# Two more layer normalisations by VectorE's batch statistics, in a fused macaron block (feed-forward, Mamba, feed-forward)

## The reference, cut to what matters

```python
x = x + 0.5 * ffn(layernorm(x))     # first feed-forward
x = x + mamba(layernorm(x))         # state-space layer
x = x + 0.5 * ffn(layernorm(x))     # second feed-forward, the same weights

def layernorm(x, eps=1e-5):
    return (x - mean(x)) / sqrt(var(x) + eps)
def ffn(x):    # 8 experts, all of them on every row
    cw = softmax(x @ w_router) * softmax(x @ w_gating / 0.1);  cw = cw / (sum(cw) + 1e-9)
    return sum_e cw[e] * ((silu(x @ w_gate[e]) * (x @ w_up[e])) @ w_down[e])   # 128 -> 512 -> 128
def mamba(x):  # 128 -> 256 inner channels, 16 states per channel
    xs, z = split(x @ W_in);  xc = silu(causal_conv4(xs) + conv_b)
    dt, B, C = projections of xc;  dt = softplus(...)
    h[t] = exp(dt[t] * A) * h[t-1] + dt[t] * xc[t] * B[t];  y[t] = h[t] . C[t]
    return ((y + xc * D) * silu(z)) @ W_out
```

## Time and profile before

| | |
|---|---|
| time, median of 3 runs | 1272.25 us (1271.98 to 1272.68) |
| span of the profiled execution | 1272.6 us |
| TensorE (PE) busy | 1253.2 us, 98% |
| VectorE (DVE) busy | 1114.1 us, 88% |
| ScalarE (ACT) busy | 926.6 us, 73% |
| GpSimd (POOL) busy | 394.3 us, 31% |

### The profile page before, as it was taken

The page is one execution under the profiler, slowest core; times in us unless marked ns, Lnnn a source line. Parts: engine busy times, 40 slices in busy tenths (PEclk is TensorE's granted clock), DMA queues, the critical chain, the costliest instruction groups (busy, mean ns, idle before and its releaser), DMA issues.

```text
span 1272.6 us, 21027 instructions
## 1 busy us (share of the span) xinstructions
PE 1253.2 (98%) x7584; PEld 1096.0 (86%) x7584; DVE 1114.1 (88%) x1481; ACT 926.6 (73%) x1778; POOL 394.3 (31%) x459
## 2 busy tenths in 40 slices
PE   7999999999999999999999999999999999999998
PEld 5888888888888888888888888888888888888887
DVE  4544899989999999999999999999999989999433
ACT  5645978978886978877968788798867968654421
POOL 0101333334342423343333433333334333332110
PEclk9999999999999999999999999999999999999999
DMA  8211677777788868787987878887978887895111
GB/s 244 52 26 30 146 155 154 147 154 158 152 180 164 170 132 183 159 165 161 180 177 150 166 164 176 158 168 148 186 157 167 163 165 142 163 183 107 35 33 33
DMA packets 109303, 182.96 MB, mean 144 GB/s; under 512 B 11024, under 2 KB 23824, under 8 KB 109200
## 3 DMA queue, kind: packets, MB, share of 16 engines
q0 software_dynamic: 56336, 102.79, 45.9%
q1 hardware_dynamic: 52864, 78.85, 24.7%
HBM read 76.22 MB, written 2.62 MB: 62 GB/s over the span
## 4 chain that ended last, share of the span: by engine, by line
PE 73%; DVE 8%; DMA 8%; issue 5%; ACT 3%; POOL 2%; SPq 0%; DVEq 0%; POOLq 0%; ACTq 0%
PE PS L700 27%; PE PS L643 14%; PE PS L646 14%; PE PS L644 14%; DMA Y<-HS 5%; DVE HB L825 2%; DVE HS L923 2%; DMA XS<-DX 2%; DVE HS L931 1%; PE PS L730 1%; PE PS L715 1%; DVE HS L912 1%; PE PS L658 1%; POOL Y L1137 1%; DVE YE L818 1%
## 5 line engine op out<-in xcount | busy, mean ns | idle before, releaser
L700 PEld LDWEIGHTS PS<-WD,HB 128*128 128x128 f32 x4096 | 536.6, 191 | 44.0 <-issue 1.5
L700 PE MATMUL PS<-WD,HB 128*128 128x128 f32 x4096 | 540.1, 275 | 0.0
L1016 ACT ACTIVATE HB<-PS 128x512 f32<-128x512 f32 x512 | 294.3, 596 | 272.9 <-PE PS L646 270.8
L825 DVE TENSOR_TENSOR HB<-PS,HB 128x512 f32<-128x512 f32 x512 | 348.7, 682 | 119.2 <-PE PS L646 110.9
L1137 POOL DMA_DIRECT2D Y<-HS x252 | 221.1, 972 | 383.7 <-DVE HS L931 262.7
L1120 POOL DMA_DIRECT2D XT<-YE x126 | 117.9, 936 | 433.2 <-DVE YE L818 407.4
L643 PE MATMUL PS<-XH,WG 128*128 128x512 f32 x512 | 244.5, 478 | 3.3 <-ACT XH L996 2.3
L643 PE MATMUL PS<-XH,WU 128*128 128x512 f32 x512 | 204.9, 400 | 0.0
L646 PE MATMUL PS<-XH,WG 128*128 128x512 f32 x512 | 203.2, 397 | 0.6 <-DVE XH L883 0.6
L646 PE MATMUL PS<-XH,WU 128*128 128x512 f32 x512 | 202.1, 395 | 0.0
L644 PE MATMUL PS<-XH,WG 128*128 128x512 f32 x512 | 201.0, 393 | 0.0
(11 more groups left out here) (109 smaller groups left out, 1080.9 us busy)
## 6 DMA issues: line engine op xcount, KB each, us to landing
BCB<-BCD SPq DMA_DIRECT2D x128, 512.0 KB, 5.3
Y<-HS POOLq DMA_DIRECT2D x252, 256.0 KB, 6.4
XT<-YE POOLq DMA_DIRECT2D x126, 256.0 KB, 4.4
XS<-DX POOLq DMA_DIRECT2D x7, 512.0 KB, 9.2
XT<-in_L_attn_x_dram SPq DMA_DIRECT2D x8, 256.0 KB, 6.5
WD<-in_L_ffn_w_down_dram SPq DMA_DIRECT2D x8, 256.0 KB, 4.8
out_dram<-XT SPq DMA_DIRECT2D x8, 256.0 KB, 5.6
HS<-in_L_ffn_w_gate_dram SPq DMA_DIRECT2D x6, 256.0 KB, 4.0
```

Of the source, the lines that this page charges most:

```text
L700: z = pe.matmul(expert(g)[:, j, :], HB[:, i % NH, j * P:(j + 1) * P], WD[:, e, c, :], start=c == 0 and j == 0, stop=c == FC - 1 and j == S ...
L825: v.tensor_tensor(H, up(i), H, ALU.mult).then_inc(S["v_h"], 1)
L1016: a.activation(HB[:, i % NH, :], gate(i), ACT.Silu).then_inc(S["a_sil"], 1)
```

## The change

`QUICK` names three normalisations: x of tile 0 (which had this form already), x1 of tile 0 (ahead of the first Mamba stage) and x2 of tile 7 (ahead of the last position). These take the form by VectorE's statistics, renamed `ln_quick` and `ln_quick_x`; the other 21 keep ScalarE's form. The quick form does not wait for `calm()` (a ScalarE clock at most 0.9 ahead of TensorE's) before it is planned. The waits are written for a quick normalisation that is not the first: VectorE waits for `a_xn` of the one before, and both writers of XN wait for what last held XN.

```diff
+QUICK = [("x", 0), ("x1", 0), ("x2", NT - 1)]
...
         yield from rows_of_x()
-        yield from calm()
-        if q == 0:
-            at = step("ln_first", b, what, after=4.0, v=1.5, p=1.2)
-            yield "first"
-            at = step("ln_first_x", b, after=at, v=.7, a=.9)
+        if what in QUICK:
+            f = QUICK.index(what)
+            at = step("ln_quick", q, f, b, what, after=clock["pe"] if q else 4.0, v=1.5, p=1.2)
+            yield True if q else "first"
+            if q:
+                yield from until_v(at - .4)
+            at = step("ln_quick_x", q, f, b, xn["by"], after=at, v=.7, a=.9)
         else:
-            at = step("ln_sum", q, b, xn["by"], what, after=clock["pe"], a=1.6)
+            f = None
+            k = q - len([w for w in QUICK if w in normed])
+            yield from calm()
+            at = step("ln_sum", k, b, xn["by"], what, after=clock["pe"], a=1.6)
             yield True
             yield from calm()
-            at = step("ln_square", q, b, after=at, a=1.6, p=2.0)
+            at = step("ln_square", q, k, b, after=at, a=1.6, p=2.0)
             yield from until(at + .3)
-            at = step("ln_x", q, b, after=at, a=1.5)
+            at = step("ln_x", k, b, after=at, a=1.5)
+        normed.add(what)
         ln["lock"] = False
...
-                        if q == 0 and j == 2:
-                            wt.wait_ge(S["v_xn"], 1)
+                        if f is not None and j == 2:
+                            wt.wait_ge(S["v_xn"], f + 1)
...
-                if k == "ln_first":
-                    _, b, what = s
+                if k == "ln_quick":
+                    _, q, f, b, what = s
                     wait_x(wt, what)
+                    wt.wait_ge(S["a_xn"], q)
                     for j in range(SUB):
                         z = v.bn_stats(stats[:, j, :], XT[:, b, j, :])
...
-                elif k == "ln_first_x":
-                    b = s[1]
-                    wt.wait_ge(S["v_nm"], 1)
+                elif k == "ln_quick_x":
+                    _, q, f, b, at = s
+                    wt.wait_ge(S["v_nm"], f + 1)
+                    wait_count(wt, at)
                     for j in range(2):
                         z = a.activation(XN[:, j, :], XT[:, b, j, :], ACT.Identity, bias=nm[:, j:j + 1], scale=rs[:, j:j + 1])
```

More of the change, by code:

```diff
@@ L90, in timetable @@
     prepared = set()
-    norms = [0]
+    norms, normed = [0], set()
     def rows_of_x():
@@ L120, in norm @@
         bk = yield from take()
-        at = step("ln_t", q, bk, pe=.6)
+        at = step("ln_t", q, f, bk, pe=.6)
         xn.update(by=("m_tr", q + 1), lock=False)
@@ L650, in _ @@
                 if k == "ln_t":
-                    _, q, (b, at) = s
+                    _, q, f, (b, at) = s
                     wait_count(wt, at)
@@ L761, in _ @@
                     v.tensor_scalar(ve[:, :], mv[:, :, 1], EPS_LN, None, ALU.add).then_inc(S["v_ve"], 1)
-                elif k == "ln_first_x":
-                    b = s[1]
-                    wt.wait_ge(S["p_rs"], 1)
+                elif k == "ln_quick_x":
+                    _, q, f, b, at = s
+                    wt.wait_ge(S["p_rs"], q + 1)
                     v.scalar_tensor_tensor(out=nm[:, :], in0=mv[:, :, 0], scalar=-1.0, in1=rs[:, :], op0=ALU.mult,
                                            op1=ALU.mult).then_inc(S["v_nm"], 1)
-                    wt.wait_ge(S["v_nm"], 1)
+                    wt.wait_ge(S["v_nm"], f + 1)
+                    wait_count(wt, at)
                     for j in range(2, SUB):
@@ L969, in _ @@
                 elif k == "ln_sum":
-                    _, q, b, at, what = s
+                    _, k, b, at, what = s
                     wait_x(wt, what)
@@ L976, in _ @@
                 elif k == "ln_square":
-                    _, q, b = s
-                    wt.wait_ge(S["a_sum"], q)
+                    _, q, k, b = s
+                    wt.wait_ge(S["a_sum"], k + 1)
                     a.activation(mean[:, :], sums[:, :], ACT.Copy, scale=-1.0 / P).then_inc(S["a_mean"], 1)
-                    wt.wait_ge(S["a_mean"], q)
+                    wt.wait_ge(S["a_mean"], k + 1)
                     for j in range(SUB):
@@ L984, in _ @@
                 elif k == "ln_x":
-                    _, q, b = s
-                    wt.wait_ge(S["p_nm"], q)
+                    _, k, b = s
+                    wt.wait_ge(S["p_nm"], k + 1)
                     for j in range(SUB):
@@ L1097, in _ @@
                 k = s[0]
-                if k == "ln_first":
-                    wt.wait_ge(S["v_ve"], 1)
+                if k == "ln_quick":
+                    f = s[2]
+                    wt.wait_ge(S["v_ve"], f + 1)
                     wt.wait_ge(S["init"], 3)
@@ L1102, in _ @@
                 elif k == "ln_square":
-                    _, q, b = s
-                    wt.wait_ge(S["a_sq"], q)
+                    _, q, k, b = s
+                    wt.wait_ge(S["a_sq"], k + 1)
                     wt.wait_ge(S["init"], 3)
                     gp.tensor_scalar(ve[:, :], squares[:, :], 1.0 / P, EPS_LN, ALU.mult, ALU.add).then_inc(S["p_ve"], 1)
-                    wt.wait_ge(S["p_ve"], q)
+                    wt.wait_ge(S["p_ve"], k + 1)
                     gp.tensor_tensor(rs[:, :], ve[:, :], mhalf[:, :], ALU.pow).then_inc(S["p_rs"], 1)
```

## The result

The changed kernel takes 1276.89 us (median of 5 runs, 1275.72 to 1277.55) against 1272.25 us for the kernel before (5 runs, 1271.13 to 1274.63): ratio 1.0037, 95% interval [1.0024, 1.0049]. That is 4.6 us slower, where 3.9 us faster was forecast, and outside the range. The span of its profiled execution is 1275.6 us against 1272.6. Wherever both are on record, the time of an execution is 1.5 to 2.0 us longer than its span (1277.16 for the span of 1275.6). So the profiled execution of the kernel before took about 1274.2 us, an estimate from its span: it is one of its longer ones, some 2 us above the median and not 0.35. Between the two profiles there are 3.0 us to explain, not 4.6.

A forecast was written before the change was run, and what follows sets the result against it. TensorE was taken as bound, with the last position's normalisation bounding a few microseconds; removing the last boundary's 3.86 us, plus 0 for x1 of tile 0 and 0 for VectorE's queue, gave 1272.25 - 3.86 = 1268.4 us, range 1265.4 to 1273.0.

The forecast's parts named there:

- the 3.86 us of the last boundary: Between positions 14 and 15: waits for XN (0.97) and XH (0.69) plus about 2.2 us of half clock, all expected to go.
- the 5.46 us of the prediction's own sum: TensorE's time without waits between the two gate products around the last boundary, summed from starts; it needed 9.32 us.
- The 2.2 us for the clock: Rest of the last boundary's cost, laid to TensorE at 1.2 GHz against 2.4 after the two pauses.
- The quick form's length and the transposes' place: x2 of tile 7: quick form takes 4.2 us, and its transposes move about one slot ahead, before the last down product.
- The cost of nothing in VectorE's queue: Some 1.3 us of statistics ahead of one product in each changed place, costed at nothing; without cover at most 1.3 each.
- The normalisation of x1 of tile 0: Ahead of the first Mamba stage: transposes 2.3 to 3.4 us earlier, later steps planned anew, effect on the total taken as zero.
- the waits that the old one shows in the middle: Bound on replanning: TensorE's 3.2 us of mid-kernel waits all gone, or as much again added.
- a sign of being wrong: Listed check: the prediction would be wrong if `s_out` starts with a wait for Y because the chain is late.
- the chain is already 0.8 us early: At `s_out` of tile 7: Y ready at 1176.03, `s_out` starts at 1176.79, so an earlier chain gains nothing directly.
- a boundary in the middle comes late: Rival, chance 0.15: a middle position's normalisation planned late, TensorE loses its clock, up to 3.86 us per boundary.
- More than the end: Rival, chance 0.14: the boundary to position 2, with 1.44 us of waits, gains another 1.4 to 2 us: 1266.7.
- The rule weighed: Whether short TensorE pauses cost clock: by the profile row, 1.4 us keeps it (1270.0); by the skill, 2.2 us may go (1272).

The follow-up runs named there:

- LATE 28: Changed kernel with LATE 28 for 26, so two more slots of position 14 may run ahead of `s_out` of tile 7: 1274.99 us, ratio 1.0024 to the kernel before.
- the last form alone: Changed kernel with the quick form for x2 of tile 7 only, x1 of tile 0 back on ScalarE: 1269.88 us, ratio 0.9986 to the kernel before.
- the form held in its old place: Changed kernel, both quick forms, but that of x1 of tile 0 planned at the places and costs of ScalarE's form: 1270.17 us, ratio 0.9989.
- half scans: Changed kernel, same order, with tile 7's scans for the last eight states over 256 of 512 columns: 1276.10 us, ratio 1.0039 to the kernel before.
- the swap alone: Kernel before, no new quick form, with the stage before tile 2's scans held until x2 of tile 0 is normalised: 1288.42 us, ratio 1.0134.

## Why the prediction was wrong

*What bounds the kernel, and the 3.86 us of the last boundary: right in kind, too large.* The waits for XN and XH and the half clock are gone from the last boundary in every profile with the quick form there, but for the one with LATE 28. Left is the 0.85 us for XH's low part, which I had called hidden beside a down product. I had looked at the copy (ScalarE) and not at what stands ahead of the low part on VectorE, a weighing that waits for that same down product. In the run with the last form alone the two gate products start at 1180.98 and 1187.71; less the 5.46 us of the prediction's own sum the boundary still costs 1.3 us. So the step is worth 2.6 us in the profiled execution; measured for the last form alone are 1.8 us (0.6 to 2.9 by its interval). The 2.2 us for the clock are not in every execution of the kernel before. Of the 57 timed beside the later runs, 15 have a mean granted clock of 0.998, as the profiled one has, and take 1273.5 us on average; the other 42, at 0.999 or 1.000, take 1271.1. The prediction took the whole 3.86 off the median. That the lower mean clock comes from this boundary is shown for the profiled execution alone.

*The quick form's length and the transposes' place: right.* From the statistics at 1184.77 to the end of VectorE's blocks at 1188.22 are 3.45 us; ScalarE's two blocks start behind a Silu at 1188.01 and end at 1188.88, 4.1 us from the start against my 4.2. The transposes stand before the last down product (1190.23 and 1190.67), one slot ahead of their old place. The cost of nothing in VectorE's queue held too, as the run with the form held in its old place shows.

*The step that failed: "The normalisation of x1 of tile 0 ... If all later stages keep that, Y of tile 7 is ready 3 us sooner ... every later step is planned anew ... I take zero."* The first half came true (transposes 3.6 us, first scan 5.2 us sooner). The rest did not. Y's last product starts 4.1 us later, and `s_out` is held 4.91 us, with 1.7 us more for its own matmuls at 1.2 GHz. The term put at zero cost about 6.5 us, by the ratios 1.0037 with both new forms and 0.9986 without that of x1. Four faults are in that step:
- I bounded the new plan by the waits that the old one shows in the middle (3.2 us, gone or doubled). The runs with one number or one condition of the planner changed lie between 0.9982 and 1.0134 of the kernel before, 19 us apart. Rows of one plan say nothing of how far another may be from it.
- I looked for the new wait at the boundaries of positions in the middle and gave it 0.15. It came in front of `s_out` of tile 7, which I had named only as a sign of being wrong, with "the chain is already 0.8 us early" as its cover. That slack was a place in a queue, not a time in hand.
- I did not print the new plan, which has a pause of 6.0 in front of that `s_out`.
- I read VectorE's full queue as a chain that arrives earlier if it starts earlier. The run with half scans shows that near the end it is tied to TensorE slot by slot.

*The rival "a boundary in the middle comes late"* had the right sign and mechanism family (a new plan, a pause, then half clock) at the wrong place: in the changed kernel the middle is no worse than before. *"More than the end"* was right on its own point, since the 1.44 us at the boundary to position 2 are gone, and was worth nothing here.

*The rule weighed:* the run with LATE 28 pauses for 2.33 us and then 0.69 at the boundary, and the granted clock is 0.50 at 1190. The run with the last form alone pauses for 0.85 there, and its clock is 1.00 from 1184 to 1192. In the changed kernel the clock is 0.50 after the 4.91 us. All three agree with the Trainium skill ("TensorE: Matmul & The Clock Gate", What's actually happening), by which the clock follows how busy TensorE has been recently. By the row I had the clock cost 2.2 us in every execution; the two groups of executions of the kernel before, 2.4 us apart, fit the other side that I had weighed, that the same pause may or may not cost it.

What stays open: why the swap alone costs as much as 1.0134 (its waits are named above, their origin in the plan is not traced), and why the planner, left alone with LEAD 2.0, plans the chain of tile 7 5.2 later than before.

## What to carry to other kernels

Where a greedy planner fixes the order of in-order engines, a cheaper step is an input to the planner and not a saving: print the order before and after, look for a place where the modelled clock of the busiest engine runs on with nothing placed, and look where a result that one engine waits for stands behind several long instructions of another with nothing to run beside them. Test an edit with the old order held, so that its own worth and that of the new order are told apart; then search the planner's numbers again for the new costs. Slack seen in one order (0.8 us here) is not slack of the dependency.

## What the runs showed of the hardware

Taking 8.5 us of work off VectorE changed the total by nothing that could be measured (1.0039 against 1.0037), although VectorE is busy 122.2 of the 125 us from 1050 to 1175 in the changed kernel (115.0 with the shorter scans): each of its short products was tied to TensorE's next slot. And a pause of 4.91 us costs TensorE more than itself: the 16 matmuls of `s_out` behind it took 3.75 us instead of 1.95, and the granted clock was 0.50 until 1184. In the five other runs with a wait of 3.77 to 8.85 us there, `s_out` took 3.50 to 3.75 us; behind the wait of 1.50 us it took 2.02.
